# A gated cross-attention and FFN stack on one core: a new order of the opening's loads, strips and staging on other queues and buffers, and a new set of planner numbers

## What is computed

```python
x = x + tanh(g_xattn[0]) * L0_xattn(layernorm(x), ctx, adj, mask)        # 16 heads of 8, additive bias adj + mask
x = x + tanh(g_ffn[0])   * L0_ffn(layernorm(x), tile_sigs, W, b)         # 8 tiles, one chosen for each token
x = x + tanh(g_xattn[1]) * L1_xattn(layernorm(x), ctx)                   # 16 heads, q/k norm, rope, causal
x = x + tanh(g_ffn[1])   * L1_ffn(layernorm(x), wi, wo, lora_A, lora_B, gate)
x = x + tanh(g_xattn[2]) * L2_xattn(layernorm(x), ctx, key mask)         # 4 query heads, 1 key/value head
x = x + tanh(g_ffn[2])   * L2_ffn(layernorm(x), Wr, W1, b1, Wo, gamma, beta)   # 8 experts 128 -> 512, gelu
x = x + tanh(g_xattn[3]) * L3_xattn(layernorm(x), ctx)                   # 16 heads
x = x + tanh(g_ffn[3])   * L3_ffn(layernorm(x), w1, w2, ...)             # adds something in batch rows 0 and 1 only
```

## Time and profile before

| | us |
|---|---|
| median of 3 runs | 1080.95 |
| lowest and highest of them | 1071.59, 1083.82 |
| the profiled execution | 1068.41 |
| its span in the trace | 1066.7 |

### The profile page before, as it was taken

One profiled execution on the slowest core, in us unless ns is written; L12 is line 12 of the kernel. 1 busy time (PEld: TensorE's weight loads), 2 busy tenths in 40 slices (PEclk: granted clock), 3 DMA queues, 4 the chain that ended last, 5 costly groups with the idle time before them and its releaser, 6 DMA issues.

```text
span 1066.7 us, 19274 instructions
## 1 busy us (share of the span) xinstructions
PE 880.5 (83%) x7316; PEld 573.0 (54%) x7316; DVE 787.8 (74%) x1849; ACT 493.7 (46%) x753; POOL 302.4 (28%) x324
## 2 busy tenths in 40 slices
PE   1778787788899998887898877787888999998686
PEld 1533346454566676663465323564456667776443
DVE  3899998778666945449778999878779574554783
ACT  2655453345534532217874656234554343322475
POOL 3600246443443211100323023655335330110000
PEclk9999777698989999988999989677998999988899
DMA  9100000000000000000110000000000000000000
GB/s 322 33 2 2 2 1 1 1 2 2 2 1 2 2 1 6 6 1 2 42 32 21 2 2 1 1 1 2 3 3 1 1 2 1 1 1 1 2 7 17
DMA packets 11741, 14.26 MB, mean 13 GB/s; under 512 B 1604, under 2 KB 10716, under 8 KB 11396
## 3 DMA queue, kind: packets, MB, share of 16 engines
q1 hardware_dynamic: 11552, 12.88, 3.7%
q10 hardware_dynamic: 100, 0.14, 0.1%
HBM read 11.55 MB, written 1.05 MB: 12 GB/s over the span
## 4 chain that ended last, share of the span: by engine, by line
PE 43%; DVE 40%; ACT 7%; issue 6%; SPq 1%; DMA 1%; POOL 1%; DVEq 0%; ACTq 0%
PE banks L986 36%; DVE nm_row L1440 13%; DVE probs L1459 5%; PE pv L986 4%; ACT probs L943 2%; DVE qf_row L1470 2%; DVE wide L1529 2%; DVE st_row L1283 2%; PE banks L682 2%; DVE xn_row L1395 1%; DVE mv_row L1285 1%; DMA xn_row<-in_ctx 1%; ACT wide L965 1%; ACT qT_row L860 1%; ACT kT_row L860 1%
## 5 line engine op out<-in xcount | busy, mean ns | idle before, releaser
L1440 DVE TENSOR_REDUCE nm_row<-banks 128x4 f32<-128x1024 f32 (+1 forms) x192 | 210.3, 1128 | 39.2 <-PE banks L986 38.6
L776 POOL TENSOR_TENSOR rstd_row<-rstd_row,neghalf 128x2 f32<-128x2 f32 x66 | 47.6, 721 | 365.8 <-DVE rstd_row L1390 277.8
L943 ACT ACTIVATE probs<-banks 128x1024 f32<-128x1024 f32 (+1 forms) x144 | 128.2, 933 | 36.5 <-PE banks L986 35.9
L986 PE MATMUL banks<-wide,c 128*128 128x256 f32 x512 | 127.9, 406 | 0.0
L986 PE MATMUL banks<-qT_row,kT_row 50*128 50x256 bf16 (+2 forms) x896 | 89.9, 298 | 29.6 <-DVE nm_row L1440 15.6
L986 PE MATMUL pv<-probs,vpad 128*32 128x256 f32 (+1 forms) x1536 | 105.7, 395 | 9.8 <-ACT probs L938 6.6
L986 PE MATMUL banks<-kT_row,qT_row 48*128 48x256 bf16 (+2 forms) x896 | 92.3, 294 | 25.7 <-DVE nm_row L1440 15.7
L986 PEld LDWEIGHTS banks<-wide,c 128*128 128x128 f32 x512 | 101.0, 202 | 18.3 <-issue 0.9
L938 ACT ACTIVATE probs<-probs 128x1024 f32<-128x1024 f32 x64 | 67.5, 1056 | 50.0 <-DVE probs L1459 48.1
L986 PE MATMUL banks<-c,wide 128*128 128x128 f32 x512 | 85.4, 336 | 3.7 <-POOL wide L834 3.7
L986 PEld LDWEIGHTS banks<-c,wide 128*128 128x128 f32 x512 | 79.6, 245 | 8.1 <-issue 6.4
(11 more groups left out here) (220 smaller groups left out, 1585.5 us busy)
## 6 DMA issues: line engine op xcount, KB each, us to landing
c<-in_c SPq DMA_DIRECT2D x1, 2500.0 KB
wide<-in_mask SPq DMA_DIRECT2D x8, 256.0 KB, 2.9
qT_row<-mT_row SPq DMA_DIRECT2D x96, 4.0 KB
c<-in_c SPq DMA_DIRECT2D x1, 1194.5 KB
xn_row<-in_ctx SPq DMA_DIRECT2D x8, 128.0 KB, 3.5
x_row<-in_x SPq DMA_DIRECT2D x8, 128.0 KB, 2.4
late<-in_late SPq DMA_DIRECT2D x2, 512.0 KB, 15.4
out<-x_row SPq DMA_DIRECT2D x8, 128.0 KB, 2.0
```

Of the source, the lines that this page charges most:

```text
L776: return pool.tensor_tensor(t, t, neghalf[:, 0:n], ALU.pow)
L943: act.activation(dst[:, :, 0:w], src[:, :, 0:w], ACT.Exp, scale=1.0 if l == 2 else HD ** -0.5).then_inc(sem["probs"], 1)
L986: return pe.matmul(dst, lhsT, rhs, start=start, stop=stop, **kw)
L1440: V.tensor_reduce(nm[b][:, t, :, 2 * jp:2 * jp + 2], ps[:, :, :, 0:kn], AX.X, ALU.max, negate=True).then_inc(sem["max"], 1)
```

## The change

SP's opening list is written in a new order. `fetch` comes ahead of `mask` in each row, so context and x of all four rows are issued first, with the masks of rows 2 and 3 between them; `adj` is cut out of `c0` and issued as a piece of its own behind the x of row 0; then come the masks of rows 1 and 0, and only behind these `consts`, which now holds the four packs alone. The strips `spreads` are issued from ACT's queue ahead of its first activation, with a semaphore of their own (`strips_in`) that PE waits for at `o_flip`. `picks` and `small` are staged in the tiles `late`, which nothing else uses in the opening, and the DMAs of `late` become a step of their own (`late`), placed ahead of level 1 of row 0. POOL waits for `adj_in` in the step `bias`. `fold` is no longer needed by level 0's `attend` and `o_flip` in the planner's dependences, and `split` is asked for by `fold` in place of `attend`. Eleven entries of `COST` and all eight of `LEAD` have new values, and `COST` has a new entry for `late`.

```diff
-    out = [("mask", 0, row), ("fetch", 0, row)] + k[0] + k[2] + k[3] + k[4] + [("bias", 0, row)]
+    out = [("fetch", 0, row), ("mask", 0, row)] + ([("consts", 0, row)] if row == ROWS - 1 else []) + k[0] + k[2] + k[3] + k[4] + [("bias", 0, row)]
     for l in range(4):
         wide = l != 2
+        out += [("late", 0, row)] if (l, row) == (1, 0) else []
...
-LEAD = [280.3, 290.2, 324.8, 314.7, 4.7, -4.1, 22.7, 13.6]
+LEAD = [296.3, 305.0, 339.6, 330.5, -5.7, 4.1, 23.0, 12.9]
...
-        ("attend", 1): [("PE", .35), ("ACT", .71), ("POOL", .6)], ("attend", 2): [("PE", .9), ("ACT", .92)],
+        ("attend", 1): [("PE", .35), ("ACT", .71), ("POOL", .6)], ("attend", 2): [("PE", .8), ("ACT", .92)],
...
-    if l >= 1 or kind in ("attend", "o_flip", "route", "choose", "spread", "outer"):
+    if l >= 1 or kind in ("route", "choose", "spread", "outer"):
...
-    if kind == "attend" and eng in ("ACT", "DVE"):
+    if kind == "late":
+        out.append((("split", 0, ROWS - 1), "DVE"))
+    if kind == "consts":
+        out += [(("mask", 0, r), "SP") for r in range(ROWS - 1)]
+    if kind == "fold" and eng in ("ACT", "DVE"):
         out.append((("split", 0, ROWS - 1), eng))
...
-        picks = probs[0][0:16, :, :].rearrange("p r n -> p (r n)"), probs[1][0:16, :, :].rearrange("p r n -> p (r n)")
-        small, rest = (t[0:3 * E, :, :].rearrange("p r n -> p (r n)") for t in (probs[2], probs[1]))
+        picks = late[0][0:16, :], late[1][0:16, 0:2 * P]
+        small, rest = late[1][0:3 * E, 2 * P:FF3], late[0][0:3 * E, :]
...
-                sp.dma_start(pack["c0"][:, :], dram["c0"]).then_inc(early_in, 16)
+                adj = WHERE["adj"][1]
+                sp.dma_start(pack["c0"][:, 0:adj], dram["c0"][:, 0:adj]).then_inc(early_in, 16)
...
+                    if kind == "late":
+                        sp.wait_ge(setup_dve, 7)
+                        for i in range(2):
+                            sp.dma_start(late[i][:, :], dram["late"][:, i * FF3:(i + 1) * FF3]).then_inc(late_in, 16)
                     if kind == "consts":
-                        sp.wait_ge(setup_zero, 1)
-                        for j in range(2):
-                            for c in range(LANES):
-                                at_row, head = COLS * c + j * (HD + 1), LANES * j + c
-                                sp.dma_start(spreads[at_row:at_row + HD + 1, :], dram["spreads"][head * (HD + 1):(head + 1) * (HD + 1), 0:P]).then_inc(const_in, 16)
                         for n in LATE_PACKS:
                             sp.dma_start(pack[n][:, :], dram[n]).then_inc(const_in, 16)
-                        for i in range(2):
-                            sp.dma_start(late[i][:, :], dram["late"][:, i * FF3:(i + 1) * FF3]).then_inc(late_in, 16)
...
+                        if row == 0:
+                            sp.dma_start(pack["c0"][:, adj:WIDTH["c0"]], dram["c0"][:, adj:WIDTH["c0"]]).then_inc(adj_in, 16)
...
                         ch.link(pool.tensor_scalar(bias, msk, 0.0, NEG, ALU.is_equal, ALU.mult))
+                        pool.wait_ge(adj_in, 16)
...
                 act.dma_start(small[:, 0:SMALL_W], dram["small"]).then_inc(picks_in, 16)
+                act.wait_ge(setup_zero, 1)
+                for j in range(2):
+                    for c in range(LANES):
+                        at_row, head = COLS * c + j * (HD + 1), LANES * j + c
+                        act.dma_start(spreads[at_row:at_row + HD + 1, :], dram["spreads"][head * (HD + 1):(head + 1) * (HD + 1), 0:P]).then_inc(strips_in, 16)
                 act.wait_ge(early_in, 16)
...
                     if kind == "o_flip" and l != 2:
+                        pe.wait_ge(strips_in, 16 * 2 * LANES)
```

More of the change, by code:

```diff
@@ L370, in place @@
                 if held is None:
-                    lines[b] += [("split", 0, row)] + begin + [("consts", 0, row)] if row == ROWS - 1 else begin
+                    lines[b] += [("split", 0, row)] + begin if row == ROWS - 1 else begin
                     lines[b] += [("fold", 0, 0)] if row == 0 else []
@@ L864, in _ @@
                         act.activation(selb[:, :], picks[0][0:E, :], ACT.Copy)
-                        act.activation(pickb[:, :], picks[1][:, 0:2 * P], ACT.Copy).then_inc(setup_act, 1)
+                        act.activation(pickb[:, :], picks[1], ACT.Copy).then_inc(setup_act, 1)
                     if kind == "fold":
```

28 lines of the change are left out of this document (15 added, 13 removed).

## The result

The kernel after takes 1083.6 us in the median of 20 runs (1077.36 to 1087.1), the kernel before, run beside it, 1075.2 (20 runs). The ratio is 1.0064, with an interval from 1.0041 to 1.0087: within 1%, but on the slow side, where the forecast was 1068.0 us. The profiled execution took 1084.97 us, its span is 1083.2.

What follows compares the result with a forecast made beforehand. PE and DVE were taken to alternate, DVE setting the pace for a hundred microseconds from the first maximum. Terms: -8.0 (parts 1 to 3) + 0.2 (part 4) + 0 (parts 5 to 7) = -7.8; 1076.2 - 7.8 = 1068 us, range 1053 to 1084.

Steps and rivals of the forecast that it cites:

- Parts 1 and 3: Opening: DVE's 8.0 us context wait goes whole; first maximum at 38.1; waits for POOL, 2.5 us, counted within 3.8 remaining.
- level 0 of the four rows done 8 us sooner: Sign of being right: the first four rows finish level 0 earlier by the opening's full net gain, 8 us.
- Part 2: DVE's fold (1.84 us) and a q_low (0.42) move behind the first maxima: work moved, not removed, 0 at the end.
- parts 1 to 3: The opening on DVE together: first maximum 10.3 us sooner, 2.3 of it owed later, 8.0 us net gain.
- Part 4: Strips issued from ACT's queue delay its table load: split starts at 9.0 to 9.5, cost 0 to 0.4 us, taken as 0.2.
- Part 5: Packs last on SP's queue: issued near 29.5, in by 44, before ACT's fold near 49; cost 0, bound 3 us.
- Part 6: The late transfers (3 us of queue), staging in other buffers and the new semaphore wait in the opening: cost 0.
- Part 7: New order of the second half, six maxima ahead of the last block: 6.8 us each way, 0, bounds -7 and +7.
- Rival A: Gain lost on the way, in PE's dense middle or the crossing to the second four rows: 1076 us, chance 0.20.
- Rival B: Slower: last row (row 4) behind the last inner sets the end, 15.9 us cost less 7.8: 1084 us, chance 0.12.
- A last block behind 980: Sign of being wrong: the last inner block begins later than 980 us of the span; 965 to 975 was expected.
- Rival C: Better order too: two slow first matmul groups and the last block's wait go, 9.0 us more: 1059 us, chance 0.18.

Runs made afterwards that it cites:

- open_only: Kernel after with the old LEAD and COST (except fetch, consts and late), so new opening with old tables: 1071.33 us, 0.9923 to the kernel before.
- tables_only: Kernel before with all of LEAD and COST from the kernel after, its old opening kept: 1084.31 us, 1.0055 to the kernel before.
- open_block_late: New opening with old tables, plus the last inner block put on PE behind all eight maxima of row 6: 1069.5 us, 0.993 to the kernel before.

## Why the prediction was right and wrong

**Parts 1 and 3, the opening: right up to the first maximum.** The wait of 8.0 us went whole, `adj` was issued at 8.29 (forecast 8.5), the first maximum came at 39.80 (38.1), and POOL's `stats` made DVE wait for 0.5 us (bound 2.5). POOL gave its first `rstd_row` at 29.18 + 0.81, not at 25.8, but DVE had asked for it late as well. The sum of -7.8 us stands against 0.9923, or 8.3 us, but that they agree is in part luck. Of the 8.0 us forecast for the end of level 0 ("level 0 of the four rows done 8 us sooner") the traces show 4.3 (164.6 to 160.3). About as much again is clock: in that session it was 0.891 in open_only's runs and 0.887 in those of the kernel before, an estimated 4 us of PE's time. On the new tables the same opening gave nothing. That the early first maximum needs the fold behind it is shown (49.80 with the fold put back).

**Part 2, the fold behind the maxima: right in place, a little small in size.** It was priced at 2.3 us owed. The runs show 3.3 (fold late, transfers as before) to 4.3 (open_only, 8.6 us at the first maximum and 4.3 at the first `mix`), so 4.3 us net where parts 1 to 3 had 8.0. The prediction also treated this part as a side effect, where it is the condition of the gain: packs last and `fold` first is worth nothing.

**Part 4: right.** `split` started at 8.63 against a forecast of 9.0 to 9.5; 0.2 us, not to be measured.

**Part 5, the packs last: right.** Issued at 32.07, 2.5 us behind the forecast of 29.5, and no engine waited for them; with the fold early they were in at 46.54, so in the kernel after ACT, asking at 52.29, had some 4 us to spare. The Trainium skill, "DMA: Bandwidth & Descriptors", "Queues, rings and completion order", has the descriptors of a queue taken in ring order. The kernel after doesn't test that: its first `shift` DMA was issued at 51.48, when the packs were in (near 48, by the 16.0 us from issue to use with the fold early).

**Part 6: no run here tries it alone.** The rest of the opening leaves nothing for it to cost.

**Part 7, the new order of the second half, priced at 0 with bounds of -7 and +7: this is the step that failed.** The new tables cost 0.55% (6 us) on the old opening and 1.4% (15 us) on the new one. I had counted the places of six maxima around one block, at 6.8 us ahead of it and 6.8 behind, and taken the sum of zero for a price; of the first half I had said only that the lists differ by one or two places. Both were the wrong thing to look at. The block's place is indeed free (0.993 with it late), but it wasn't what mattered. And in the first four rows 288 of PE's steps have another place, some by up to 11; moving two leads by 1, which changes about as many (275), costs 1.4% by itself. What the runs show in its place is two losses of the whole order: longer waits of DVE at the blocks (87.4 to 98.8 us in all) with 5 us more idle time of PE in the tail, and a lower clock of PE (0.881 for 0.891 in the means of all runs, an estimated 10 us). Which steps of the order bring the lower clock stays open. The bound of 7 us had no term for the clock.

**Rival A, the gain is lost on the way: its time, 1076, wasn't measured, but what it describes did happen with the new tables.** Against tables_only, which has the same tables, the kernel after is 3.9 us ahead when level 0 is done, 1.3 when the first four rows are done and 0.1 at the last `mix`. With the old tables open_block_late is 5.0 us ahead of the kernel before (159.6 for 164.6) and 5.4 at the crossing (543.6 for 549.0), so there the crossing doesn't eat it. Why it does once and not the other time is open.

**Rival B, slower, the last row behind the last block: its sign was right and its time, 1084, was the measured one. Its mechanism fell.** It was to decide when the last block begins later than 980; it began at 994.5. Yet open_block_late puts it at 986.3 and stays at 0.993, and the kernel after with the block early (982.8) stays slow; open_only's own block begins at 981.96. "A last block behind 980", which the prediction names as a sign of being wrong, is none. Nor was it the exchange of rows 4 and 5: with it undone the kernel after measures 1.0052.

**Rival C, a better order: it didn't come.** The two slow first groups stand at 6.17 us (954.62) and 6.54 (994.84) where they were 6.40 and 6.46. The Trainium skill, "TensorE: Matmul & The Clock Gate" (Part 1), which was cited for it, has an idle PE start its next burst at half rate. The rows of before agree with it (6.46 us behind a wait of 3.58), but in the kernel after the group is as slow (6.54) behind a wait of only 0.83, in a stretch whose mean clock was 0.76 already; the wait directly ahead doesn't price it.

**What stays open.** Why one order gives PE a lower clock than another: the low pieces follow PE's idle pieces in the rows above, but no run changed the clock without the order. One and the same kernel spreads widely: the twelve runs of open_only go from 1064.9 us at a mean clock of 0.899 to 1081.0 at 0.886. How much of the opening's 0.8% is the opening is open too. A nudge of the tables moved the kernel by 1.4%, and with the new transfers only three orders near the old one were tried: with the last block late (0.993) and with rows 6 and 7 exchanged (0.9928) they kept the gain, with the first four leads new (0.9994) it was gone. And whether the new tables have any merit that another chip or another opening would show was not tried. The best kernel measured is open_only, 0.9923, ahead of both.

## What to carry to other kernels

Where a table of numbers steers a planner, a new fit is not a small change to be priced at zero: time it apart from the edit that it comes with, and time a purposeless nudge of one number too, since here a nudge of 1 cost as much as the whole fit. Before a run, compare the planner's own end for the two orders, and count how many steps change their place in each list: both said here that the nudge was no small change. In an order written for several engines, look at each long block of one engine, and at what the other has ready beside it; the place of the last block alone told nothing. Look also for a short step that stands behind one that waits for the block, like ACT's `divide` above. And when transfers are put first, look for the step that will wait for those that are now last; moved with them it is the condition of the gain, left in place it takes all of it. Last, follow a gain through the stages: one that agrees with the forecast at the end can be half of it where it was made.

## What the runs showed of the hardware

- With the same 7316 matmuls, PE's busy time in the profiles goes from 880.5 us (before, mean clock 0.902) to 909.9 (after with the last leads old, 0.874), 29 us more. A good part of that can be the execution alone: open_only, with the orders of the kernel before from level 1 on, was busy for 899.8 us at 0.886 in its longest run.
- The length of the wait directly ahead of a block doesn't tell how slow its first group is: the group at 994.84, behind a wait of 0.83 us, took 6.54 us, as much as the one in the earlier trace rows that follows a wait of 3.58 (6.46). In the stretch ahead of that block PE was busy for 13.24 of 20 us, and at a mean clock of 0.76 already. The kernel after, around its last block:

```profile
969.70:989.70 20.00, 13.24 (x118) 9.44 (x117) 13.04 (x26) 7.73 (x10) 0.70 (x1) 0.76 0.00 0
989.70:1009.70 20.00, 18.31 (x69) 12.75 (x68) 5.79 (x10) 1.51 (x3) 1.38 (x2) 0.73 0.01 2
```

- The four packs, issued at 30.56 and used at 46.54, moved 5.13 MB in at most 16.0 us, 321 GB/s or more, near the 350 of the earlier trace rows.
